# One DRAM row per product row: packing split q and k with three transfers per tile, loading them with four transfers per step

## The reference

```python
x = x + attn_a(layernorm(x))     # 16 heads of 8, elu+1, rotary numerator, plain denominator
x = x + ffn(layernorm(x))        # shared expert + 8 experts, top 2
x = x + attn_b(layernorm(x))     # state space scan, 16 states
x = x + ffn(layernorm(x))        # the same weights again

# attn_a, cut to what the change touches
q = elu(q) + 1; k = elu(k) + 1
attn_num   = einsum('bhid,bhjd->bhij', rope(q), rope(k))
attn_denom = einsum('bhid,bhjd->bhij', q, k)
out = einsum('bhij,bhjd->bhid', attn_num / attn_denom, v)
```

## Time and profile before

| | |
|---|---|
| median of 3 timed runs | 4204.29 us (4202.71 to 4212.35) |
| the profiled execution's own time | 4196.47 us |
| its span | 4194.5 us |
| TensorE busy | 84% of the span |
| ScalarE busy | 77% |
| VectorE busy | 69% |
| GpSimd busy | 36% |
| mean granted clock of TensorE | 0.916 of full speed |
| DMA queue, share of 16 engines | 39.5% |
| DMA packets | 184390, 526.88 MB |

### The profile page before, as it was taken

How to read it: one execution, slowest core, us unless ns; L and a number is a source line. 1 busy time by engine, 2 the same in 40 slices (tenths; PEclk the granted TensorE clock), 3 DMA queues, 4 the chain that set the end, 5 groups by cost and what they waited for, 6 DMA issues and landing times.

```text
span 4194.5 us, 39166 instructions
## 1 busy us (share of the span) xinstructions
PE 3514.4 (84%) x11446; PEld 1492.4 (36%) x11446; DVE 2902.8 (69%) x3513; ACT 3228.1 (77%) x4037; POOL 1500.8 (36%) x758
## 2 busy tenths in 40 slices
PE   3877598988889898988889898898989888898857
PEld 1131243433333343333334333333334333333423
DVE  2426568768686767868686777858677786858592
ACT  2667588887888787888878888888878888786653
POOL 1112244435243443524344342524434252414361
PEclk9586699999999999999999999999999999998977
DMA  3131244444444444444443444434444444434432
GB/s 120 37 120 58 96 127 147 134 140 129 133 135 126 137 140 130 132 130 136 129 143 122 144 130 131 137 124 141 129 138 133 132 139 133 129 109 135 133 122 86
DMA packets 184390, 526.88 MB, mean 126 GB/s; under 512 B 19217, under 2 KB 66162, under 8 KB 184178
## 3 DMA queue, kind: packets, MB, share of 16 engines
q1 hardware_dynamic: 184178, 524.38, 39.5%
HBM read 488.65 MB, written 38.01 MB: 126 GB/s over the span
## 4 chain that ended last, share of the span: by engine, by line
PE 42%; DVE 16%; ACT 13%; issue 11%; DMA 10%; SPq 7%; POOL 1%; ACTq 0%; POOLq 0%; DVEq 0%
PE bank L782 13%; DMA bc<-bcscr 6%; PE bank L771 4%; PE bank L673 4%; PE bank L734 4%; ACT L1022 4%; ACT rPool L884 3%; SPq L583 3%; DMA kpk<-kscr 3%; PE bank L773 3%; PE bank L712 3%; PE bank L772 3%; DVE ws L1220 3%; SPq L584 3%; PE bank L707 3%
## 5 line engine op out<-in xcount | busy, mean ns | idle before, releaser
L782 PE MATMUL bank<-hF,wst 128*128 128x512 f32 x2304 | 1200.8, 637 | 39.5 <-DVE tmp L1178 34.0
L884 ACT ACTIVATE hF<-bank,cols 128x512 f32<-128x512 f32 x1152 | 770.6, 686 | 362.4 <-PE bank L773 352.7
L1108 DVE TENSOR_TENSOR rPool<-bank,rPool 128x512 f32<-128x512 f32 x1024 | 699.7, 683 | 500.6 <-PE bank L712 470.5
L1313 POOL TENSOR_TENSOR acc<-acc,tmp 128x512 f32<-128x512 f32 x240 | 428.0, 1783 | 1300.3 <-DVE tmp L1178 1297.7
L1328 POOL TENSOR_TENSOR yM<-yM,ws 128x1024 f32<-128x1024 f32 x240 | 699.7, 2915 | 485.1 <-DVE ws L1227 474.4
L884 ACT ACTIVATE rPool<-bank 128x512 f32<-128x512 f32 x1040 | 573.9, 594 | 254.4 <-PE bank L707 202.8
L771 PE MATMUL bank<-xnH,wst 128*128 128x512 f32 x1152 | 648.3, 563 | 90.0 <-ACT hF L884 69.0
L1022 ACT ACT_TABLE_LOAD x531 | 681.3, 1283 | 9.4
L1220 DVE TENSOR_TENSOR_SCAN ws<-dAs,ws 128x1024 f32<-128x1024 f32 x256 | 674.9, 2636 | 5.9 <-ACT dAs L884 3.4
L712 PE MATMUL bank<-qpk,kpk 48*128 48x512 bf16 x1024 | 424.4, 414 | 257.0 <-DVE rPool L1108 255.7
L782 PEld LDWEIGHTS bank<-hF,wst 128*128 128x128 f32 x2304 | 423.3, 199 | 466.1 <-issue 365.3
(11 more groups left out here) (154 smaller groups left out, 3064.2 us busy)
## 6 DMA issues: line engine op xcount, KB each, us to landing
wst<-wscr SPq DMA_DIRECT2D x288, 768.0 KB, 5.9
bc<-bcscr SPq DMA_DIRECT2D x256, 512.0 KB, 4.1
cB<-gscr SPq DMA_DIRECT2D x256, 256.0 KB, 4.8
qscr<-parts SPq DMA_DIRECT2D x32, 384.0 KB, 9.6
kscr<-parts SPq DMA_DIRECT2D x32, 384.0 KB, 3.0
kpk<-kscr SPq DMA_DIRECT2D x128, 96.0 KB
qpk<-qscr SPq DMA_DIRECT2D x128, 96.0 KB
kpk<-kscr SPq DMA_DIRECT2D x128, 64.0 KB
```

The source lines that it names most:

```text
L782: pe.matmul(ps[FFN][:, :], w2, hF[:, q % HSLOTS, :], start=(c == 0), stop=(c == FC - 1)).then_inc(s_dn, 1)
L884: return nc.scalar.activation(out_, in_, fn, **kw)
L1108: v.tensor_tensor(rP[:, step % 2, c, :], ps[NUM][:, :], rP[:, step % 2, c, :], ALU.mult).then_inc(s_mul, 1)
```

## The change

The scratch gets six rows, one for each product, instead of three, one for each part. The packing of a tile becomes three transfers that write each part as many times as it occurs: for q the parts 0, 0, 0, 1, 1, 2 (a broadcast source), for k the parts 0, 1, 2, 0, 1, 0. `load_heads` then reads all six rows with one transfer for each of k and q and each `u`, four for each call. The source of this load has the channel `d` as its outermost dimension and the product row inside it (8, 6, 2048), so on the 48 partitions channel `d` of product `r` now lies at 6d + r instead of 8r + d, for q and k alike. Waits on `s_pk` count three transfers for each tile, and `LOADS` is 2.

```diff
--- before.py
+++ after.py
@@ -40,7 +40,8 @@
 G_AHEAD = {"w": 8, "up": 26, "gelu": 24, "down": 20, "part": 5, "add": 5, "gate": 7}
 HALF = 64
 USED = HD * 6
-LOADS = 6
+LOADS = 2
+REPEATS = ((0, 0, 3), (3, 1, 2), (5, 2, 1))
 
 HEAD = {
     "SP": """
@@ -272,8 +273,8 @@
         ps = [ctx.enter_context(nc.psum_tensor(f"bank{i}", [P, 512], F32)) for i in range(8)]
         NUM, AV, PRE, UP, FFN = 2, 3, 4, 5, 7
 
-        qscr = nc.dram_tensor("qscr", (NB, 2, PARTS, P, 512), BF16, kind="Internal").ap()
-        kscr = nc.dram_tensor("kscr", (NB, 2, PARTS, P, 512), BF16, kind="Internal").ap()
+        qscr = nc.dram_tensor("qscr", (NB, 2, 6, P, 512), BF16, kind="Internal").ap()
+        kscr = nc.dram_tensor("kscr", (NB, 2, 6, P, 512), BF16, kind="Internal").ap()
         wscr = nc.dram_tensor("wscr", (NE + 1, P, 3, FF), F32, kind="Internal").ap()
         gscr = nc.dram_tensor("gscr", (2 * NB, NE, 512), F32, kind="Internal").ap()
         bcscr = nc.dram_tensor("bcscr", (NB, NS, 2, 512), F32, kind="Internal").ap()
@@ -487,6 +488,7 @@
         N_CONST, N_PCONST = 7, 2
         N_ROUTE, N_EOP = 19, 6
         N_DTX = 3
+        N_PK = 16 * len(REPEATS)
 
         def f_first(i):
             return 0 if isinstance(i, int) and i == 1 else 2 * i - 3
@@ -563,25 +565,29 @@
                     n, u = divmod(t, 2)
                     sp.wait_ge(s_A_split, floor(16 * b + 4 * (t + 1)))
                     settled(sp)
-                    scratch = qscr if n == 0 else kscr
-                    sp.dma_start(scratch[b, u].rearrange("a p t -> p a t"), parts[:, u, :, :]).then_inc(s_pk[u], 16)
+                    scratch = (qscr if n == 0 else kscr)[b, u].rearrange("r p t -> p r t")
+                    for r, part, many in REPEATS:
+                        if n == 0:
+                            src = parts[:, u, part:part + 1, :].broadcast_to([P, many, 512])
+                        else:
+                            src = parts[:, u, 0:many, :]
+                        sp.dma_start(scratch[:, r:r + many, :], src).then_inc(s_pk[u], 16)
 
             def load_heads(b, k):
                 if k == 0:
-                    sp.wait_ge(s_pk[0], floor(32 * (b + 1)))
+                    sp.wait_ge(s_pk[0], floor(N_PK * 2 * (b + 1)))
                     settled(sp)
-                    sp.wait_ge(s_pk[1], floor(32 * (b + 1)))
+                    sp.wait_ge(s_pk[1], floor(N_PK * 2 * (b + 1)))
                     settled(sp)
                 sp.wait_ge(s_num, floor(UNITS * b + JB * NC * (k - 1)))
                 settled(sp)
                 heads = slice(HALF * (k % 2) + 32 * (k // 2), HALF * (k % 2) + 32 * (k // 2) + 32)
                 for u in range(2):
-                    qs = qscr[b, u, :, heads, :].rearrange("a (d c) t -> a d (c t)", c=NC)
-                    ks = kscr[b, u, :, heads, :].rearrange("a (d c) t -> a d (c t)", c=NC)
-                    for r, part, many in ((0, 0, 3), (3, 1, 2), (5, 2, 1)):
-                        here = slice(HALF * u + HD * r, HALF * u + HD * (r + many))
-                        sp.dma_start(kpk[here, k % 2, :], ks[0:many]).then_inc(s_k_ld[k % 2], 16)
-                        sp.dma_start(qpk[here, k % 2, :], qs[part:part + 1].broadcast_to([many, HD, NC * 512])).then_inc(s_q_ld[k % 2], 16)
+                    here = slice(HALF * u, HALF * u + USED)
+                    ks = kscr[b, u, :, heads, :].rearrange("r (d c) t -> d r (c t)", c=NC)
+                    qs = qscr[b, u, :, heads, :].rearrange("r (d c) t -> d r (c t)", c=NC)
+                    sp.dma_start(kpk[here, k % 2, :], ks).then_inc(s_k_ld[k % 2], 16)
+                    sp.dma_start(qpk[here, k % 2, :], qs).then_inc(s_q_ld[k % 2], 16)
 
             def ffn(f, name, e):
                 if name == "w":
@@ -916,7 +922,7 @@
                     act.wait_ge(s_A_rope, floor(6 * b + 3 * (t // 2) + 3))
                     act.wait_ge(s_A_split, floor(16 * b + 2 * n))
                     if part == 0:
-                        act.wait_ge(s_pk[slot], floor(16 * (2 * b + t // 2)))
+                        act.wait_ge(s_pk[slot], floor(N_PK * (2 * b + t // 2)))
                     a(parts[:, slot, part, :], til[:, t, :], ACT.Copy).then_inc(s_A_split, 1)
 
             def att(b, name, n):
```

## The result

The changed kernel takes 4023.16 us (median of 4 runs, 4020.63 to 4026.42), the kernel before, timed with it, 4203.5: a ratio of 0.957, 95% interval 0.955 to 0.959, or 180 us less. The forecast was 4060, 143 us less. The profiled execution took 4020.79 us.

The account below looks back on a forecast made before the run. No engine is full; waits for slow loads and the `bc` queued behind them lengthen the pass. 33 us at the start plus 110 in 13 passes, 143 us, gave 4060 us (80% range 3995 to 4150).

Parts of the forecast that it names:

- The loads spread over 8 engines, and this is the gain: Loads of q and k: 8 engines instead of 3.5, 173 GB/s instead of 76, a burst in 4.5 us instead of 10.3.
- Four issues at 1.03 us: SyncE's queue: four loads at 1.03 us each, 4.1 us a burst, 3.3 us less than now; bounds 0.63 and 1.23.
- The packing costs nothing in the steady state and 1.5 us at each of three places: Three packing transfers per tile: covered in the steady state; 1.5 us in each of the first three passes, without cover.
- the three long waits: TensorE's waits of 37.93, 18.06 and 22.14 us at the start and first two boundaries, each forecast about 6 us shorter.
- The start and first boundaries, 33 us: Start and first two boundaries: three waits at 6 us, a next-input wait 6, a wait behind `bc` 9; 33 us saved.
- The steady state, 8.5 us a pass: Steady passes: 6.3 us from the `bc` stall and its low clock, 2.2 from `kpk` at half; 110 us over 13.
- the 84.4 us: VectorE's waits for `bc` without the longest, 10.44 us: 6.5 us in each of 13 passes.
- What is late next: Behind the removed `bc` stall: the following `bc` load, waiting for its buffer, lands late and leaves a new 2 us wait.
- The loads spread no better: Rival, 6%: on the loads only 3.3 us of issue a burst are saved; 43 us at most, likely half, 4180 us.
- slower through packing: Rival, 4%: late packing makes `P.ahead` 0 block SyncE; at 40 us of landing, 15 us a pass lost, 4256 us.
- Other waits take half of it: Rival, 18%: in steady passes the next waits grow after the stall is gone; half the gain, 70 us, 4130 us.
- more than counted: Rival, 9%: SyncE less busy, `wst`, `cB` and `bc` earlier, the mid-pass clock dip gone; another 5 us a pass, 3995 us.

Follow-up runs that it names:

- e1: Kernel before with the channel outermost in the source of each of its twelve loads, so all use 8 engines, nothing else changed; 4030.37 us, ratio 0.958.
- e2: Changed kernel with each load cut in two halves of three rows, product row outermost: 3 engines, eight issues a burst; 4128.22 us, ratio 0.9815.
- e4: Changed kernel with a scratch where a load's 48 rows are one run (16 engines), six packing transfers per tile; 4019.92 us, ratio 0.9561 to the kernel before.
- e3: Kernel before with only the packing changed: six-row scratch, three packing transfers, its twelve loads reading the six rows; 4208.22 us, ratio 1.0002.
- e6: Changed kernel with the product row instead of the channel outermost in the load's source: four loads on 6 engines; 4029.79 us, ratio 0.9597.
- e7: Changed kernel with two words exchanged in VectorE's steady-pass list, an expert's eviction ahead of the multiplication by C; 4020.85 us, ratio 0.9574.

## Why the prediction was right, step by step

**The loads spread over 8 engines, and this is the gain.** Right, shown by e1 (spread alone, 175 of 180 us); e2 agrees in part, with the long stall still there on 3 engines, but keeps 77 us. The DMA share of 0.52 in the quiet stretch is the 8 of 16 engines that was taken, and 167 GB/s the 173 of the sum. The rule of the Trainium skill on how a transfer is spread ("DMA: Bandwidth & Descriptors", section "Why a DMA increments its semaphore by 16 and not by 1") gives 3, 6, 8 and 16 engines for the forms tried. The trace agrees, with 2.7, 5.9, 8.3 and 15.2 busy engines; in e1, where the queue sets the pace, it has 4.8 and can't show the 8. The fit that the prediction took from the Trainium skill ("DMA: Bandwidth & Descriptors", section "Anatomy of one DMA") is given there for transfers issued from GpSimd; these are SyncE's, so the trace doesn't test it. The prediction's upper bound, 16 engines at 21.6 GB/s each or 346 GB/s, is far off: e4 reached 198.

**Four issues at 1.03 us.** Too high: 0.64 to 0.68 (the burst above), near the low bound of 0.63. So the step from 16 to 24 rows was a price neither for each row nor for each engine. The burst saves 4.7 us of the queue, not 3.3; e1 against the changed kernel shows that it matters little once the data is quick. And `bc` isn't issued 3.3 us earlier, as the sum had it, but 1.2, because its buffer isn't free before. The stall went all the same: `bc` is read at 1818.45, 7.6 us after its issue instead of 12.0, and VectorE waits there for GpSimd.

**The packing costs nothing in the steady state and 1.5 us at each of three places.** Right in the time: at the start the loads begin 1.2 us later (67.41 for 66.19), and e3 is within 0.1% of the kernel before by the medians. At the three long waits e3's leads are -1.5, -3.3 and -4.7 us, 1.5 to 1.8 for each; its profiled execution loses another 4.7 us ahead of pass 2, where one more wait for `bc` stands, and 0.3 a pass. There are 25,341 more packets, 24,600 were forecast. On the queue a packing issue took 0.49 us at the median, not 0.37, so three cost 1.1 us more than one instead of 0.75, which nobody waited for.

**The start and first boundaries, 33 us.** Right in sum, partly by luck. The matmul that began at 473.35 behind the third boundary now begins 33.3 us earlier:

```profile
440.02 0.60 PE L718 MATMUL bank<-qpk,kpk 48*128 48x512 bf16 x1 [3.15 <-DVE rPool L1114]
```

So 33 forecast and 33.3 measured. By the leads the three long waits give 5.4, 4.0 and 5.3 us where 6 each were taken, the next input 6.0 (6 taken), and the stall behind `bc` 6.1 (9 taken). That these add up is due to a wait that the sum didn't have, TensorE's for expert weights (`wst`) behind the second boundary. Before, and in the changed kernel, which gains 6.2 us there:

```profile
243.92 0.80 PE L771 MATMUL bank<-xnH,wst 128*128 128x512 f32 x1 [6.64 <-DMA wst<-wscr]
```

```profile
222.32 0.79 PE L777 MATMUL bank<-xnH,wst 128*128 128x512 f32 x1 [0.49 <-DMA wst<-wscr]
```

From the first load to the first score 7 us were forecast and 7.9 measured.

**The steady state, 8.5 us a pass.** This term was too small: 10.8, or 140 us over 13 passes where the sum had 110. Where it arises can be read from the leads, here in the pass of the earlier trace rows (starts on TensorE, both timelines):

| TensorE instruction, line before / now | before | changed | lead, us |
|---|---|---|---|
| output projection, L740 / L746 | 1894.12 | 1807.85 | 86.3 |
| last one ahead of the stall, L707 / L713 | 1906.90 | 1820.65 | 86.3 |
| first behind it, L712 / L718 | 1913.17 | 1820.93 | 92.2 |
| behind the low clock, L673 / L679 | 1919.27 | 1824.47 | 94.8 |
| behind the new wait, L712 / L718 | 1923.32 | 1832.47 | 90.9 |
| ahead of the half of the pass, L712 / L718 | 2006.73 | 1914.87 | 91.9 |
| at the half, L707 / L713 | 2008.90 | 1914.89 | 94.0 |
| ahead of `P.ahead` 0, L782 / L788 | 2100.07 | 2006.10 | 94.0 |
| next output projection, L740 / L746 | 2134.46 | 2039.38 | 95.1 |

On the mean of passes 2 to 13 the place of the long stall gives 5.6 us of waiting and 2.4 of clock (5.88 and 2.4 forecast), and 2.9 are lost again behind it (2.0 forecast): 5.1 instead of 6.3. The half of the pass gives 2.5 us of waiting, as forecast (2.2), and 1.2 more of clock: in nine of the twelve passes the stretch behind it gets quicker by 1.6 us (one of them: granted clock 0.72 from 1767 to 1773 before, 1.00 from 1685.6 to 1691 now). `P.ahead` 0 gives 2.0 us where the sum had nothing.

At this last place VectorE had waited for `bc` in seven of 13 passes, 1.2 to 2.5 us each. The prediction had these waits among the 84.4 us and counted nothing for the place. They are gone, and with them part of a stretch at the lower clock level, 1.2 GHz. The window behind that place, in the kernel before and in the changed one (the clock is the number after the five engines):

```profile
1871.00:1881.00 10.00, 9.15 (x17) 2.23 (x18) 7.47 (x5) 5.88 (x8) 4.28 (x2) 0.50 0.21 84
```

```profile
1785.00:1795.00 10.00, 9.01 (x30) 2.39 (x31) 9.94 (x9) 7.99 (x10) 8.71 (x3) 0.66 0.31 114
```

And the stall's low clock is shorter: the earlier trace rows had 0.53, the same work now runs at 1.00, and 0.76 follows in 1826 to 1833, where the prediction had no dip any more. Over the span the mean clock rose from 0.916 to 0.929.

**What is late next.** Its size was near, its mechanism wrong. I had VectorE wait 2 us for a `bc` load that waits for its buffer. That load had been issued one buffer earlier (1814.98, above; 1901.24 in the kernel before, where the one at 1917.11 is for the state after it); no such wait exists. The 2.19 us stand on TensorE, because VectorE, no longer held up, is the one that is full; another 1.7 us go to the lower clock behind this wait (the 0.76 above), and 1.0 comes back later. The changed kernel's VectorE in this stretch:

```profile
1818.45 1.23 DVE L1222 TENSOR_TENSOR ws<-bc,dtx 128x1024 f32<-128x1024 f32 x1 [0.91 <-POOL yM L1334]
...
1820.79 3.27 DVE L1226 TENSOR_TENSOR_SCAN ws<-dAs,ws 128x1024 f32<-128x1024 f32 x1
1823.98 0.66 DVE L1114 TENSOR_TENSOR rPool<-bank,rPool 128x512 f32<-128x512 f32 x1
1824.56 2.72 DVE L1233 TENSOR_TENSOR ws<-bc,ws 128x1024 f32<-128x1024 f32 x1
1827.21 0.74 DVE L1184 SCALAR_TENSOR_TENSOR tmp<-bank,cols,cB 128x512 f32<-128x512 f32 x1
1827.87 1.62 DVE L1222 TENSOR_TENSOR ws<-bc,dtx 128x1024 f32<-128x1024 f32 x1
```

The scan takes 3.27 us and the multiplication by C 2.72, with no gap between any two of them, and the eviction (L1184) comes last. GpSimd adds beside it:

```profile
1815.97 10.23 POOL L1334 TENSOR_TENSOR yM<-yM,ws 128x1024 f32<-128x1024 f32 x3
```

In the kernel before, GpSimd did these three additions faster, most of it while VectorE was stalled, and VectorE's two operations ran alone after it:

```profile
1913.03 2.28 DVE L1220 TENSOR_TENSOR_SCAN ws<-dAs,ws 128x1024 f32<-128x1024 f32 x1
...
1915.81 1.21 DVE L1227 TENSOR_TENSOR ws<-bc,ws 128x1024 f32<-128x1024 f32 x1
...
1902.24 7.37 POOL L1328 TENSOR_TENSOR yM<-yM,ws 128x1024 f32<-128x1024 f32 x3
```

**The rivals.** "The loads spread no better" is excluded by the share at the start and by e1; "slower through packing" by e3. "Other waits take half of it" didn't occur, but its kind did, with 2.9 us a pass, and so did "more than counted", with 2.3 us a pass instead of 5. Not tried is whether four issues without more engines would have done as well: by e2 part of the gain, but not the long stall.

## What to carry to other kernels

Read how many DMA engines a small transfer really uses: busy share times 16 in a stretch where it runs alone. If it is far below 16, look at the outermost dimension on both sides before merging or shrinking anything; here turning two dimensions round (e1) gave 175 of 180 us without a byte less or an issue less. Six engines were enough (e6), three weren't (e2). A slow transfer costs through what is queued behind it as well: in the steady state before, VectorE waited 84 us for `bc` and TensorE 31 us for `kpk` itself. Once it is through before its successors are needed, making it faster still brings nearly nothing (8 to 16 engines: 3 us, within the noise). When a stall is removed in a list ordered by hand, look first whether the engine that follows has any gap left; where it had none, exchanging its work brought nothing (e7). And compare two traces instruction by instruction: sums that agree can hide terms that don't.

## What the runs showed of the hardware beyond this

A load of 48 rows of 4 KB takes no longer to issue than one of 16 rows (0.64 to 0.63 us), and in e4, where both sides are plain two-dimensional patterns, 0.33 to 0.42. VectorE's scan of 128x1024 takes 2.3 us with GpSimd idle and 3.0 on the mean with GpSimd at work beside it all the time, its product of the same size 1.2 and 2.2. Loads of 48 such rows, alone in flight, moved 167 GB/s on 8 engines and 198 on 16, 20 and 13 for each engine.
